# Local attention pipeline on one core: the turning of the feed-forward's rows placed in the next step

## What is computed

```python
def _layer(x, wqkv, qs, ksc, wo, lg, lb, w1, b1, w2, b2):      # for each of DEPTH = 2
    h = shift_token(x)                     # half of the columns from the row before
    q, k, v = split(h @ wqkv)              # 8 heads of 64
    q, k = rotary_xpos(l2norm(q) * qs, l2norm(k) * ksc)
    o = local_attention(q, k, v)           # windows of 64 rows, each sees itself and the one before
    x = x + o @ wo
    h = shift_token(x)
    h = (h - mean(h)) / sqrt(var(h) + 1e-05) * lg + lb
    a, g = split(h @ w1 + b1)
    return x + (a * gelu(g)) @ w2 + b2
```

## Time and profile before

| | us |
|---|---|
| median of three runs | 1997.1 |
| lowest and highest | 1995.74, 1999.32 |
| the profiled execution | 1997.87 |
| its span | 1996.1 |

### The profile page before, as it was taken

The page is one execution under the profiler, slowest core; times in us unless marked ns, Lnnn a source line. Parts: engine busy times, 40 slices in busy tenths (PEclk is TensorE's granted clock), DMA queues, the critical chain, the costliest instruction groups (busy, mean ns, idle before and its releaser), DMA issues. The chain is left out here.

```text
span 1996.1 us, 54360 instructions
## 1 busy us (share of the span) xinstructions
PE 1788.1 (90%) x23072; PEld 1112.9 (56%) x23072; DVE 1442.8 (72%) x2638; ACT 1441.5 (72%) x1755; POOL 1408.5 (71%) x797
## 2 busy tenths in 40 slices
PE   5999999999999999999999999758899999778936
PEld 1466666666666666666666666745555666333523
DVE  5787787777777877878777764258888887244774
ACT  1688888888888888888888899228888888422422
POOL 3689999999899899899899899747655556022000
PEclk8899999999999999999999999879999999768968
DMA  4100101101101001011010000501111111000000
GB/s 114 29 22 25 29 18 29 29 18 29 25 22 29 22 25 29 18 29 29 18 29 24 19 10 2 169 17 40 37 38 34 35 35 30 5 1 0 1 0 22
DMA packets 71018, 56.59 MB, mean 28 GB/s; under 512 B 29164, under 2 KB 64312, under 8 KB 70776
## 3 DMA queue, kind: packets, MB, share of 16 engines
q1 hardware_dynamic: 70776, 53.11, 10.5%
HBM read 14.21 MB, written 1.05 MB: 8 GB/s over the span
## 5 line engine op out<-in xcount | busy, mean ns | idle before, releaser
L304 POOL TENSOR_TENSOR ah_probs_lo<-ah_probs,ah_probs_hi 128x1024 f16<-128x1024 f32 x512 | 1080.5, 2133 | 130.6 <-ACT ah_probs L496 130.6
L553 DVE TENSOR_REDUCE ah_part_max<-ah_p_m 128x1 f32<-128x512 f32 x1024 | 682.4, 686 | 184.4 <-PE ah_p_m L368 169.1
L493 ACT ACTIVATE ah_probs_hi<-ah_p_s 128x1024 f16<-128x1024 f32 x512 | 523.7, 1023 | 181.5 <-PE ah_p_s L387 160.7
L496 ACT ACTIVATE ah_probs<-ah_p_s 128x1024 f32<-128x1024 f32 x512 | 521.4, 1018 | 0.0
L401 PE MATMUL ah_p_o<-ah_v_hi,ah_probs_hi 128*128 128x65 f16 x4096 | 476.6, 195 | 34.3 <-DVE a_attn L568 28.9
L405 PE MATMUL ah_p_o<-ah_v_hi,ah_probs_lo 128*128 128x65 f16 x4096 | 476.1, 194 | 0.0
L403 PE MATMUL ah_p_o<-ah_v_lo,ah_probs_hi 128*128 128x64 f16 x4096 | 476.0, 193 | 0.0
L401 PEld LDWEIGHTS ah_p_o<-ah_v_hi,ah_probs_hi 128*128 128x128 f16 x4096 | 383.0, 98 | 140.8 <-DVE a_attn L568 59.8
L403 PEld LDWEIGHTS ah_p_o<-ah_v_lo,ah_probs_hi 128*128 128x128 f16 x4096 | 378.5, 98 | 96.9
L368 PE MATMUL ah_p_m<-ah_k_hi_lo,ah_q_hi_twice 128*128 128x512 f16 x1024 | 393.8, 385 | 5.4 <-DVE ah_part_max L553 5.0
L386 PE MATMUL ah_p_s<-ah_q_hi_twice,ah_k_hi_lo 128*128 128x512 f16 x1024 | 389.1, 380 | 0.3 <-ACT ah_probs L496 0.3
(11 more groups left out here) (280 smaller groups left out, 3135.9 us busy)
## 6 DMA issues: line engine op xcount, KB each, us to landing
ba_v_skew<-ba_v_own SPq DMA_DIRECT2D x64, 129.0 KB, 2.4
ah_q_hi_twice<-ah_hi SPq DMA_DIRECT2D x128, 64.0 KB, 2.0
ah_k_hi_lo<-ah_hi SPq DMA_DIRECT2D x64, 64.0 KB, 1.9
ah_one_k_hi<-ah_hi SPq DMA_DIRECT2D x64, 64.0 KB, 2.0
ah_k_hi_lo<-ah_lo SPq DMA_DIRECT2D x64, 64.0 KB, 2.0
ah_max_q_lo<-ah_lo SPq DMA_DIRECT2D x64, 64.0 KB, 2.0
ah_w_head<-in_w_heads SPq DMA_DIRECT2D x16, 160.0 KB, 2.5
bw_rot<-in_rot SPq DMA_DIRECT2D x4, 512.0 KB, 11.0
```

Of the source, the lines that this page charges most:

```text
L304: pool.tensor_tensor(pl[:, p % RW, :, :], pb[:, p % RP, :, :], ph[:, p % RW, :, :], ALU.subtract).then_inc(lo_pool, 1)
L493: act.activation(ph[:, p % RW, :, :], p_s[:, p % 2, :, :], ACT.Exp, scale=HD ** -0.5)
L496: act.activation(pb[:, p % RP, :, :], p_s[:, p % 2, :, :], ACT.Exp, scale=HD ** -0.5).then_inc(exp_done, 1)
L553: dve.tensor_reduce(part[:, t, 2 * half + b:2 * half + b + 1], p_m[:, b, :], AX, ALU.max).then_inc(maxed, 1)
```

## The change

The turning of the feed-forward's rows and its eviction are taken from the end of step j (tile j-6) and put into the next one (tile j-7, j being one more). PE does it after the projection of q and k and before the transposed scores, VectorE after the two rotation products and before the sum of squares. The waits are the same with their numbers moved by one step. `project_v` is untouched: its wait for the eviction of tile u-7 now falls on an eviction of the same step.

```diff
--- before.py
+++ after.py
@@ -1198,6 +1198,16 @@
                 for j in range(-2, STEPS_B):
                     if on(j):
                         project_qk(j)
+                    u = j - 7
+                    if on(u):
+                        pe.wait_ge(h2n_done, u + 1)
+                        if on(j):
+                            pe.wait_ge(hTl_done, j + 1)
+                        if on(j - 1):
+                            pe.wait_ge(vl_done, j)
+                        if u >= 1:
+                            pe.wait_ge(hT2_done, u)
+                        pe.transpose(p_e[:, P:2 * P], h2n[:, u % 2, :], ident[:, :]).then_inc(h2_turned, 1)
                     if on(j - 2):
                         scores_turned(j - 2)
                     if on(j):
@@ -1222,16 +1232,6 @@
                         scores_for_max(j - 1)
                     if on(j - 3):
                         out_project(j - 3)
-                    u = j - 6
-                    if on(u):
-                        pe.wait_ge(h2n_done, u + 1)
-                        if on(j + 1):
-                            pe.wait_ge(hTl_done, j + 2)
-                        if on(j):
-                            pe.wait_ge(vl_done, j + 1)
-                        if u >= 1:
-                            pe.wait_ge(hT2_done, u)
-                        pe.transpose(p_e[:, P:2 * P], h2n[:, u % 2, :], ident[:, :]).then_inc(h2_turned, 1)
                     feed(j, 2)
 
             @block.scalar
@@ -1356,6 +1356,17 @@
                                               x4.unsqueeze(1).to_broadcast([P, 2, HEADS_B, DH]),
                                               lw.tab[:, u // NT, u % NT, s, :, :].unsqueeze(2).to_broadcast([P, 2, HEADS_B, DH]),
                                               ALU.mult).then_inc(done, 1)
+                    u = j - 7
+                    if on(u):
+                        m, i = divmod(u, GROUP)
+                        l = u // NT
+                        dve.wait_ge(h2_turned, u + 1)
+                        if u == 0:
+                            dve.wait_ge(lw.ff_in, lw.FF)
+                        if m >= 2:
+                            dve.wait_ge(a_ready, HC * (m - 1))
+                        dve.tensor_scalar(hT2[:, m % 2, i * P:(i + 1) * P], p_e[:, P:2 * P], lw.gb[:, l, 0:1],
+                                          lw.gb[:, l, 1:2], ALU.mult, ALU.add).then_inc(hT2_done, 1)
                     u = j
                     if on(u):
                         dve.wait_ge(squared, 2 * u + 2)
@@ -1449,17 +1460,6 @@
                         if u >= NT:
                             dve.wait_ge(xo_done, t // GROUP + 1)
                         dve.tensor_tensor(xm[:, t, :], p_o[:, 1, 0:D], x_in(u)[:, t, :], ALU.add).then_inc(xm_done, 1)
-                    u = j - 6
-                    if on(u):
-                        m, i = divmod(u, GROUP)
-                        l = u // NT
-                        dve.wait_ge(h2_turned, u + 1)
-                        if u == 0:
-                            dve.wait_ge(lw.ff_in, lw.FF)
-                        if m >= 2:
-                            dve.wait_ge(a_ready, HC * (m - 1))
-                        dve.tensor_scalar(hT2[:, m % 2, i * P:(i + 1) * P], p_e[:, P:2 * P], lw.gb[:, l, 0:1],
-                                          lw.gb[:, l, 1:2], ALU.mult, ALU.add).then_inc(hT2_done, 1)
                     hidden(j, 2)
                     m, r = geglu_of(j)
                     if r == 3:
```

## The result

| | us |
|---|---|
| before, median of four runs | 1996.42 |
| changed, median of four runs | 2026.70 |
| lowest and highest | 2024.67, 2027.03 |
| ratio, 95% interval | 1.0157 (1.0137 to 1.0176) |
| the profiled execution, its span | 2024.67, 2022.8 |

The change makes the kernel slower by 30 us, 1.6%. The forecast was slower, 2018 us, with a range up to 2034. Profiles are of one execution each; that of the change is the shortest of its four.

A forecast was written before the change was run, and what follows sets the result against it. A ring of ScalarE and TensorE work was taken to bound the steps, VectorE beside it. Step terms of 15 us and 6 for the clock on the profiled 1997.87 gave 2018.9, the median 0.8 lower: 2018 us, range 2005 to 2034.

The forecast's parts named there:

- The new wait: Before v's projection in steps 7 to 31, TensorE waits for VectorE's eviction: 1.0 to 1.2, 1.7 or near 3.9 us.
- Kind 3: Steps whose number minus 10 leaves rest 3 by 4 (13 to 29): K to K 10.82 against 10.42 us, +0.40.
- Kind 2: Steps whose number minus 10 leaves rest 2 by 4: K to K 12.58 against 12.63 us, taken as 0.
- K: Start of ScalarE's copy of the turned keys (L1283), the mark of a step; K to K is a step's length.
- Kind 0: Steps whose number minus 10 leaves rest 0 by 4 (10 to 30): 11.65 against 10.76 us, +0.89; step 10 +0.3.
- Steps 7 to 9: Steps without a feed-forward piece between v's projection and K: 10.05 us, about what they take, so 0.
- From step 32 on: Steps where no v projection waits: taken as 0, within 1 us either way.
- Kind 1: Steps whose number minus 10 leaves rest 1 by 4 (11 to 31): K to K 15.43 against 14.00 us, +1.43.
- The clock: TensorE's slower clock around the long wait before v's projection: up to 2.6 us, taken as 1.0 in each of six steps.
- The removed wait is the gain: Rival: TensorE's 17.3 us of waiting for h_norm come back, giving 1980 us, or 1988 with half; chance 0.08.
- Cover: Rival: gains left out balance the later v projection, leaving the time within 0.2%, 4 us; chance 0.03.
- later still: Rival: rotation products start no earlier (2035 us), or slow-clock stretches cover more work (2028, up to 2040); chance 0.14.

The follow-up runs named there:

- The kernel before, filled: The kernel before, plus 5 added TensorE matmuls of 128x512 ahead of the first feed-forward piece in steps with rest 1: 1993.97 us, ratio 0.9990.
- the run with the wait filled: The change, plus 16 never-read TensorE matmuls during the wait for the eviction in steps with rest 1: 2017.48 us, ratio 1.0118.
- the run that evicts twice: The change, with the eviction made twice, the second behind the end of the first: 2042.03 us, ratio 1.0239.
- the run that evicts first: The change, but VectorE evicts the turned rows ahead of the two rotation products: 1980.69 us, ratio 0.9936, and 0.9926 when run again.

## Why the prediction held, step by step

*The new wait.* Its place (v's projection, released by the eviction), its number (25) and its lengths were forecast as 1.0 to 1.2, 1.7 and 3.9 us, and measured as 1.12, 1.72 and 3.93. That the eviction's place behind the products costs more than the removed wait gives was shown by two runs: with the eviction ahead of the products the kernel gains 13 to 15 us, and with the late eviction but the turning in its old place it loses 45.

*Kind 3*: forecast 10.82, measured 10.82.

*Kind 2*: 12.58, measured 12.67. The size is right, but most of the gain in it had another source than the one given. The products start 6.89 us after K in place of 8.14, 1.25 us earlier. The prediction put that down to VectorE's catching up. The kernel before, filled, has no slow stretch in this kind, and there they start at 7.31: so 0.83 us of the gain is the slow stretch that is gone from this kind, and only 0.42 the catching up. At the same clock the change costs 0.9 us in a kind-2 step (12.67 against 11.79) and not 0. Step 12 shows it without an added matmul: no slow stretch fell there in the kernel before, its first gate pair took 1.12 us, and the step 11.77; with the change it takes 12.65. This step is 0.9 of the 1.1 us of loss in this kind.

```profile
1446.52 1.12 PE L1177 MATMUL ba_p_h<-ba_h2T,bw_w 128*128 128x512 f32 x2 [0.27 <-DVE ba_hiddenT L1337]
```

*Kind 0*: 11.65, measured 11.71; the total was 5.7 against 4.8 forecast. *Steps 7 to 9*: forecast 0, measured -0.1. *From step 32 on*: forecast 0, within 1 us; it was -1.2 in step 32, of which 0.8 is a slow stretch that the kernel before had there.

*Kind 1*: without the clock the forecast was 15.43, and the run with the wait filled has 15.56; the third gate product starts 4.35 us after K in place of the forecast 4.25. With the clock, 15.4 to 16.4 was named as the sign of being right, and a period of 50.5 to 51.5. Both were missed: the kind-1 steps took 17.0 to 18.15, and the period shown above 53.4.

*The clock.* This is the term that was mis-sized: "I take 1.0 in each of six steps, 6 us", a choice below the middle of nothing and 2.6 us. In the profiles it measured 1.85 us a step, 11.1 us, about midway between the 1.0 and the prediction's own bound of 2.6; by the medians it is 8 us. In every step the slow stretch fell on the work behind the wait, at least in part: two of the six steps took 18.1 us, 2.5 and 2.6 us above the filled run's 15.56, and the other four 17.0 to 17.2, 1.4 to 1.6 above it. Against this stand the 4.1 us that the kernel before had lost by its own slow stretches and the change did not; the 3.3 us of them that fall in kind 2 are in the prediction's number for that kind, under another name. Of the 8.7 us by which the median is above the forecast, 5.7 stand between the two profiled executions, and 5.1 of these are this term; the rest is which executions are compared. The Trainium skill, "TensorE: Matmul & The Clock Gate", Part 1, says that the clock follows how busy the engine was lately; the filled run agrees, with 3.23 against 5.82 us for the same work.

*The rivals.* "The removed wait is the gain" is true of another kernel: where the eviction is done while the scores still run, that is ahead of the products, the time falls to 1981 us, which the rival's 1980 to 1988 had. The prediction's decision point for it, an R 1.0 us earlier, was about right: with the eviction one product (1.1 us) earlier kinds 2 and 3 no longer wait. "Cover" did not come about. Of "later still" only one part did, a slow stretch over all the work from V to the turning, in two of the six kind-1 steps.

*The range.* Its lower end does not follow from its words: 2018 without the clock's 6 us and with half of -1.8 us in five kind-2 steps is 2007.5, not 2005. Nothing hangs on it.

## What to carry to other kernels

When a step of an in-order engine is moved, look for every wait elsewhere that names its semaphore: here an untouched line (v's projection) waited for the moved eviction, and it was queued ahead of most of TensorE's step. Place such an eviction ahead of the long work on its engine, even where it must wait a little for its input; what counts is whether it ends before the consumer's previous work does, and beyond that point each tenth of a microsecond is paid, as the run that evicts twice shows. And add to a forecast stall on TensorE a cost for the work that follows at once, between nothing and the full half-speed cost; here, behind 3.93 us, it was 1.4 to 2.6 us of 2.6. Look also at whether the kernel before has slow stretches of its own, since a change can move them.

## What was not expected of the hardware

A stall's clock cost was as large as a good part of the stall itself: in step 19, 3.93 us of waiting made the next 3.23 us of work take 5.82. The stretches are also touchy. The kernel before stood still 1.11 us, and 0.81 us after the next K, in each period and had a slow stretch in five of six periods; the run that evicts first stood still 1.00 and 0.81 us at the same places and had one in two of six periods in one profile (12.54 in place of 11.9 in step 20, 10.50 in place of 9.78 in step 32) and in one of six in the other (12.27 in step 32). With the eviction twice, a wait of 2.2 us in kind 0 was enough for a second slow stretch in some periods.
